# Deformable-convolution block on one core: 45 near taps, batched far columns, and an earlier silu

## The chip, the cores and the metric

The kernel runs on one core of one Trainium2 chip. The metric is the device time of one execution in microseconds (us); of several runs the median counts. The engines are called PE (TensorE), DVE (VectorE), ACT (ScalarE), POOL (GpSimd) and SP (SyncE, which here issues the large DMAs).

## The reference, cut to what matters

The block is a deformable convolution with a residual, then attention, then a mixture of experts. Only the first part is touched. For every pixel, each of 8 groups of 16 channels and each of 9 points, a small network gives an offset (x, y) and a softmax weight; the projected image is sampled at the shifted place with bilinear weights, and the 9 samples are added.

```python
N, H, W, C = (4, 32, 32, 128)
G, K = (8, 3)
P = K * K
...
x1 = jax.nn.silu(x1)
...
offset = x1 @ off_w + off_b
mask = jax.nn.softmax((x1 @ mask_w + mask_b).reshape(N, H, W, G, P), -1)
...
samples = _bilinear_sample(img, sg)
m = mask.reshape(N, H * W, G, P).transpose(0, 2, 1, 3).reshape(N * G, 1, H * W, P)
out = (samples * m).sum(-1)
...
return out @ out_w + out_b
```

## The kernel before

**Tiling.** The image is worked in 8 chunks (`CHUNKS`) of 4 rows (`ROWS`). A partition is one (column, image) pair, 32 by 4 = 128 of them, so a chunk has 4 rows times 8 groups = 32 places per partition.

**Near points as a stencil.** An offset of at most 2 pixels (`REACH`) moves a sample inside a window of 7 by 7 taps (`WIN`, `STENCIL` = 49). `prepare` (ACT) copies the offsets out of PSUM, squares them for the far test, and makes `hats`, the bilinear weight of each point on 5 taps in x and in y. DVE weighs the y hats with the softmax weights (`weigh_hats`), and in `stencils` multiplies them out for each of 9 points (`outer`, 800 elements) and adds that into the 7 by 7 stencil (800 elements). Then `products` (DVE) multiplies shifted copies of the image by the stencil, tap by tap, two taps in one instruction (a *unit*: 1024 elements, or 512 for the odd tap of each row; 28 units a chunk), into 7 slots of `prod`, and PE adds each tap up with 4 transposing matmuls (`add_up`).

**One turn.** DVE's `turn(k)` runs the products of chunk k as filling between the dependent steps of chunk k+1: `finish_silu`, `mask_logits`, `masks`, `weigh_hats`, 9 outer products and 8 additions. `own.wait()` in front of a step waits for DVE's own earlier results; `fill(n)` puts n units between. PE's `turn` puts into the taps, by their number, the count of far points (`AT_FAR`), the convolution of chunk k+2 (`AT_CONV`), the far part (`AT_SAMPLES`) and the projection (`AT_PROJECT`). All orders are written by hand.

**Far points.** A (row, group, point) column of a chunk in which any of the 128 partitions has an offset over 2 is *far*. DVE flags them (`off_most`, `far_flags`), PE counts them (`count_far`), ACT copies the counts (`count_out`), DVE lists up to 8 with one MAX8 (`list_far`), and POOL goes through the list in a loop of 7, column by column (`add_point`): position, cell, 4 indirect DMAs, weights, and the sum into `fix`. PE adds `fix` with `add_fix`.

**What ties POOL to the rest.** `list_far(k)` waits for `list_taken` = k, which POOL raises after the cast and the `place` update with which it begins chunk k-1, so after it has ended chunk k-2; and for `far_done`, which comes from `count_out(k)` on ACT, which waits for `fix_done`, also the end of chunk k-2. `fix_done` begins at 2, to let the first two through. `list_far(k+1)` stands in the DVE's `turn(k)`. PE's `add_fix(k-1)` stands in its `turn(k)` and waits for the end of POOL's chunk k-1.

Of the kernel before, what the change touches and what calls it, by code (L numbers as in the profile page):

```python
# [21 lines left out]
ALU = mybir.AluOpType  # L22
# [8 lines left out]
P = 128  # L31
# [24 lines left out]
ROW_UNITS = -(-WIN // 2)  # L56
UNITS = WIN * ROW_UNITS
# [28 lines left out]
FAR_UNIT = 8192.0  # L86

# [6 lines left out]
def first_of(unit):  # L94

    return unit // ROW_UNITS * WIN + unit % ROW_UNITS * 2
# [32 lines left out]
def hybrid_block_kernel(nc, x, in_w, in_b, out_w, out_b, off_w, off_b, mask_w, mask_b, dw_k, bn_g, bn_b,  # L129
                        bn_m, bn_v, attn_w, wr, br, w1, b1, w2, b2, gamma, beta, out):  # L130
    padded = nc.dram_tensor("padded", (WP, B, HP, C), F32, kind="Internal").ap()
    with ExitStack() as ctx:
# [3 lines left out]
        def sem(name):  # L136
# [24 lines left out]
        bias_parts = sb("bias_parts", [1, 3, 3 * GP + C], BF16)  # L161
# [23 lines left out]
        off_most = sb("off_most", [P, ROWS * GP])  # L185

        far = sb("far", [P, FAR_COLS], BF16)
        far_flags = far[:, :]
# [5 lines left out]
        far_xy = outer[:, :, :, :].rearrange("p g a b -> p (g a b)")[:, 0:ROWS * 2 * GP] \  # L194
            .rearrange("p (r o) -> p r o", r=ROWS)
# [27 lines left out]
        pos = sb("pos", [P, 2])  # L223
        low = sb("low", [P, 2])
        frac = sb("frac", [P, 2, 2])
        stride = sb("stride", [P, 2])
        cell_at = sb("cell_at", [P, 2])
        corner = sb("corner", [P, 4])
        cell_f = sb("cell_f", [P, 4])
        cell_now = sb("cell_now", [P, 4], U32)  # L230
        w_now = sb("w_now", [P, 2, 2])
        side = sb("side", [P, 2, 2])
        tap_d = sb("tap_d", [P, 2])
        tap_c = sb("tap_c", [P, 2, 2])
        within = sb("within", [P, 2, 2])
        got_sum = sb("got_sum", [P, 2, CG])
        got = sb("got", [P, 4, CG])
# [80 lines left out]
        square_done = sem("square_done")  # L318
# [14 lines left out]
        masks_done = sem("masks_done")  # L333
# [7 lines left out]
        gathered = sem("gathered")  # L341
# [75 lines left out]
        def _(sp):  # L417
# [62 lines left out]
            for k in range(HALF):  # L480
                s0, s1 = ROWS * k, (ROWS * (k + 1) if k < HALF - 1 else SLOTS)
                sp.wait_ge(prod_done, (k + 1) * STENCIL)
# [46 lines left out]
        def _(sc):  # L529
# [35 lines left out]
            def prepare(k):  # L565
# [10 lines left out]
                sc.activation(far_xy, raw[:, :, 0:2 * GP], ACT.Square).then_inc(square_done, 1)  # L576
# [15 lines left out]

            def copy_out(k):
# [12 lines left out]
            def clear_stencil(k):  # L606

                sc.wait_ge(prod_done, (k + 1) * STENCIL)
# [13 lines left out]
            prepare(0)  # L622
            count_out(0)
            silu(1)
            prepare(1)
            count_out(1)
            silu(2)
# [127 lines left out]
        def _(pe):  # L755
# [31 lines left out]
            def offsets(k):  # L787
                pe.wait_ge(x1_done, k + 1)

                pe.wait_ge(fold_done, 1)  # L790
                if not isinstance(k, int) or k > 0:
                    pe.wait_ge(square_done, k)
                for r in range(ROWS):
# [3 lines left out]
                mm.then_inc(off_mm, 1)  # L797
# [15 lines left out]
            for q in range(CHUNKS):  # L813
# [3 lines left out]
                if q == 2:  # L817
                    keep_clock(4, pair[0][:, 512:1024])
                    pe.wait_ge(bias_in, 16)
                    offsets(0)  # L820
# [11 lines left out]
            def count_far(k):  # L832

                pe.wait_ge(masks_done, k + 1)
# [3 lines left out]
                count = pair[1][:, 0:FAR_COLS]  # L838
                pe.matmul(count, ones16[:, :], far[:, :], start=True, stop=False)
                pe.matmul(count, ones[0:1, :], far_codes[:, :], start=False, stop=True).then_inc(far_mm, 1)  # L840
# [4 lines left out]
            def add_up(k, first, last):  # L845

                for i in range(first, last):
                    c, d = k + i // STENCIL, i % STENCIL
                    pe.wait_ge(prod_done, c * STENCIL + d + 1)
# [898 lines left out]
```

## Time and profile before

| | value |
|---|---|
| median of 3 runs | 697.59 us (697.52 to 699.57) |
| the profiled execution's own time | 699.83 us |
| its span | 698.0 us |
| busy, share of the span | PE 593.9 us (85%), DVE 583.2 us (84%), POOL 318.7 us (46%), ACT 227.5 us (33%) |
| DVE's first far list | at 61.2 us |
| DVE's turns begin | 63.88, 115.14, 165.22, 215.40, 265.80, 316.29, 366.50 us |
| last product of the convolution part | ends at 442.7 us |

The beginning of a turn is the start of its `finish_silu` (L1337). From 442.7 us on the kernel is the attention and expert part, whose code is the same in both kernels. A share of busy time over the whole span is a mean over those parts; for the change the turns have to be read alone.

### The profile page before, as it was taken

How to read it: one execution, taken by the hardware profiler on the slowest of the kernel's cores; microseconds unless marked ns; L12 is line 12 of the kernel's file. 1: busy time of each engine (PE TensorE's matmuls, PEld its weight loads, DVE VectorE, ACT ScalarE, POOL GpSimd, SP SyncE). 2: the span in 40 equal slices, each digit the busy share in tenths (PEclk: the TensorE clock that was granted, in tenths of full speed). 3: DMA queues.
4: the chain of work that ended last, by engine and by line, in shares of the span. 5: the costliest groups of instructions: out<-in, count | busy, mean ns of one | idle time of the engine just before them, and what ended most of it. 6: DMA issues, size and time to landing. Idle time of an engine off the chain costs nothing.

```text
span 698.0 us, 11520 instructions
## 1 busy us (share of the span) xinstructions
PE 593.9 (85%) x3630; PEld 444.2 (64%) x3630; DVE 583.2 (84%) x1068; ACT 227.5 (33%) x335; POOL 318.7 (46%) x332
## 2 busy tenths in 40 slices
PE   5988877879868968878878679889999999989995
PEld 4557656557556556556566557557777777776674
DVE  4589999999999999999999999816767776654877
ACT  6150502414314216107016000234454544424431
POOL 7507795897727795168278240201221211124322
PEclk9899999999999999999989899989999999999998
DMA  7096303003003006000000000000000000004211
GB/s 189 31 353 212 109 0 107 2 1 108 2 0 108 1 3 263 1 1 2 1 1 3 0 1 1 0 1 0 1 2 1 0 1 1 1 1 107 54 38 46
DMA packets 25724, 30.57 MB, mean 44 GB/s; under 512 B 5316, under 2 KB 17812, under 8 KB 25684
## 3 DMA queue, kind: packets, MB, share of 16 engines
q1 hardware_dynamic: 24094, 29.77, 13.1%
q0 software_dynamic: 896, 0.23, 0.4%
q8 instruction: 29, 0.48, 0.3%
q10 hardware_dynamic: 694, 0.01, 0.1%
q14 instruction: 11, 0.09, 0.0%
HBM read 24.94 MB, written 5.05 MB: 43 GB/s over the span
## 4 chain that ended last, share of the span: by engine, by line
PE 48%; DVE 25%; issue 12%; DVEq 2%; ACT 1%; DMA 0%; SPq 0%; POOL 0%; ACTq 0%; POOLq 0%
DVE prod L1481 11%; PE banks L851 11%; PE banks L967 8%; PE pair L947 8%; DVE outer L1418 4%; PE pair L1025 4%; DVE stencil L1424 4%; PE banks L957 4%; PE banks L1063 4%; PE pair L802 3%; PE pair L795 2%; PE banks L873 1%; DVEq L1481 1%; PE banks L939 1%; PE banks L918 1%
## 5 line engine op out<-in xcount | busy, mean ns | idle before, releaser
L851 PE MATMUL banks<-ident,prod 128*128 128x128 f32 x1568 | 222.9, 288 | 72.4 <-DVE prod L1481 70.1
L851 PEld LDWEIGHTS banks<-ident,prod 128*128 128x128 f32 x1568 | 184.0, 148 | 132.2 <-DVE prod L1481 108.2
L1481 DVE TENSOR_TENSOR prod<-shifted,stencil 128x1024 f32 (+1 forms) x224 | 238.2, 1086 | 5.3 <-PE banks L851 5.3
L1249 POOL TENSOR_TENSOR rstd_now<-mv_now,neg_half 128x2 f32<-128x2 f32 x32 | 23.0, 718 | 133.8 <-DVE mv_now L1533 133.8
L802 PE MATMUL pair<-xg,dw_diag 128*128 128x512 f32 x144 | 73.2, 609 | 0.3 <-DVE xg L1303 0.3
L1221 POOL CAST far_list_i<-far_list 1x8 int32<-1x8 f32 x8 | 33.7, 4217 | 74.9 <-DVE far_list L1467 47.0
L967 PEld LDWEIGHTS banks<-shifted 128*128 128x128 f32 x512 | 60.2, 192 | 8.1 <-issue 6.1
L967 PE MATMUL banks<-shifted 128*128 128x128 f32 x512 | 63.3, 277 | 2.3 <-ACT shifted L683 1.4
L947 PE MATMUL pair<-shifted 128*128 128x512 f32 x128 | 61.6, 604 | 0.7 <-ACT shifted L666 0.6
L1548 DVE TENSOR_REDUCE neg_max<-pair 128x1 f32<-128x1024 f32 x32 | 39.2, 1225 | 23.7 <-PE pair L947 22.6
L1418 DVE TENSOR_TENSOR outer<-hats 128x800 f32<-128x800 f32 x56 | 55.2, 986 | 0.5
L1424 DVE TENSOR_TENSOR stencil<-stencil,outer 128x800 f32 (+1 forms) x56 | 55.0, 982 | 0.0
L1186 POOL DMA_INDIRECT got<-padded,cell_now x28 | 45.4, 1621 | 8.4 <-issue 6.4
L585 ACT ACTIVATE hats<-off,tap_bias 128x576 f32 (+1 forms) x40 | 48.4, 1339 | 0.0
L678 ACT ACTIVATE shifted<-pair,neg_max 128x1024 f32<-128x1024 f32 x32 | 35.7, 1115 | 34.2 <-DVE neg_max L1548 34.2
L1553 DVE COPY shifted<-banks 128x512 f32<-128x512 f32 x32 | 22.0, 689 | 23.2 <-PE banks L957 23.2
L957 PE MATMUL banks<-ident,shifted 128*128 128x128 f32 x256 | 34.1, 277 | 0.0
L947 PEld LDWEIGHTS pair<-shifted 128*128 128x128 f32 x128 | 22.2, 193 | 17.4 <-issue 15.9
L1255 POOL TENSOR_TENSOR res<-res,bias_all 128x256 f32 x16 | 11.6, 728 | 46.2 <-DVE xg L1539 46.2
L558 ACT ACTIVATE gate<-pair,bn_fold 128x512 f32<-128x512 f32 x8 | 6.2, 774 | 79.7 <-issue 66.3
L957 PEld LDWEIGHTS banks<-ident,shifted 128*128 128x128 f32 x256 | 30.2, 144 | 1.3 <-issue 0.2
L1025 PE MATMUL pair<-shifted,stage 128*128 128x512 f32 x64 | 29.3, 597 | 1.4 <-DMA stage<-in_L_ffn_W_dram 1.4
(238 smaller groups left out, 895.0 us busy)
## 6 DMA issues: line engine op xcount, KB each, us to landing
shifted<-padded SPq DMA_DIRECT2D x42, 256.0 KB
shifted<-padded SPq DMA_DIRECT2D x14, 640.0 KB
res<-in_x_dram SPq DMA_DIRECT2D x4, 512.0 KB, 6.2
padded<-stage SPq DMA_DIRECT2D x4, 512.0 KB, 11.0
stage<-in_L_ffn_W_dram SPq DMA_DIRECT2D x16, 128.0 KB, 2.3
out_dram<-res SPq DMA_DIRECT2D x16, 128.0 KB, 1.8
padded<-stencil SPq DMA_DIRECT2D x2, 228.0 KB, 2.5
got<-padded,cell_now POOLq DMA_INDIRECT x28
```

The source lines that it names most:

```text
L585: own(sc.activation(hats[:, :, :, t].rearrange("p a (r g) -> p a r g", r=ROWS), off[:, bass.ds(k % OFFS, 1), :, 0:2 * GP].rearrange("p s r ...
L802: mm = pe.matmul(conv_bank.rearrange("c (r a) -> c r a", r=ROWS), dw_diag[:, t, :], src, start=(t == 0), stop=(t == 8))
L851: mm = pe.matmul(acc_of(c, r), prod[:, d % PROD, r * G:(r + 1) * G, :].rearrange("p g c -> p (g c)"), ident[:, :], is_transpose=True, star ...
L947: mm = pe.matmul(pair[s][:, h * 512:(h + 1) * 512], keyed[:, bass.ds(i * P, P)], normed_t[:, bass.ds((i // TILES) * TOK + h * 512, 512)], ...
L957: mm = pe.transpose(bank[h][:, m * P:(m + 1) * P], probs[:, s, (4 * h + m) * P:(4 * h + m + 1) * P], ident[:, :])
L967: mm = pe.matmul(bank[2][:, 0:C], probs_t[:, m * P:(m + 1) * P], normed[:, bass.ds((i // TILES) * TILES + m, 1), :].rearrange("p t c -> p ...
L1025: pe.matmul(pair[j][:, (f % 2) * 512:(f % 2 + 1) * 512], w1_sel[:, 2 * (q // 2) + j, (f % 2) * P:(f % 2 + 1) * P], normed2_t[:, q * 512:(q ...
L1186: gp.indirect_dma_start(out=got[:, a, :], out_offset=None, in_=table, in_offset=bass.IndirectOffsetOnAxis(ap=cell_now[:, a:a + 1], axis=0) ...
L1418: own(ve.tensor_tensor(to if q == 0 else outer[:, :, :, :], hy[:, :, q, :].unsqueeze(3).to_broadcast(full), hx[:, :, q, :].unsqueeze(2).to ...
L1424: own(ve.tensor_tensor(to, to, outer[:, :, :, :], ALU.add))
L1481: ins = ve.tensor_tensor(prod[:, dx:dx + n, :, :], shifted[:, dx:dx + n, bass.ds(((c % HALF) * ROWS + dy) * G, ROWS * G), :], stencil_of[: ...
L1548: ve.tensor_reduce(neg_max[:, s:s + 1], pair[s][:, :], AX.X, ALU.max, negate=True).then_inc(max_done, 1)
```

## The change

- **Taps**: the four corner taps of the window are dropped: 45 taps (`NEAR`) in a new order of rows (`ROW_ORDER`), 26 units a chunk instead of 28. A point whose weight falls on a corner tap now counts as far, and POOL's weights take it over.
- **Flags**: DVE's `off_most`, `far_flags` and ACT's square are gone. ACT makes two sign maps (`signs_of`), DVE two small instructions for the corners (`corners`), and PE's `count_far` sums them in six matmuls where two were. The four subtractions of the row maximum become one.
- **POOL**: columns are worked in batches of up to 4 (`add_batch`): take each, cells for all, gather each, weights for all, collect each. An absent column of a batch is skipped by a branch, but `cells` and `corner_weights` run once in a batch whatever its number. Further batches are skipped if empty.
- **Order**: `finish_silu` of the chunk after next moves from the turn's beginning into the stencil steps; the offsets of that chunk are computed at the end of PE's turn, so ACT begins the hats before the turn ends. `hats_used` is raised before the last addition. All but two additions are followed at once by an outer product, and two units stand behind each outer product. `list_far` stands one point earlier, `add_fix` at tap 21 in place of 35.

DVE, in `turn`, around the far list (L1418/L1526 is the outer product, L1424/L1534 the addition, L1481/L1591 a unit, MAX the far list, L1439 `finish_silu`). Before:

```order
L1418 TENSOR_TENSOR outer<-hats 128x800
L1481 TENSOR_TENSOR prod<-shifted,stencil 128x512
L1424 TENSOR_TENSOR stencil<-stencil,outer 128x32x5x5
L1481 TENSOR_TENSOR prod<-shifted,stencil 128x1024
L1467 MAX far_list<-pair 1x8
L1418 TENSOR_TENSOR outer<-hats 128x800
L1481 TENSOR_TENSOR prod<-shifted,stencil 128x1024
L1424 TENSOR_TENSOR stencil<-stencil,outer 128x32x5x5
```

DVE, the same place in the changed kernel:

```order
L1534 TENSOR_TENSOR stencil<-stencil,outer 128x32x5x5
L1578 MAX far_list<-pair 1x8
L1526 TENSOR_TENSOR outer<-hats 128x800
L1591 TENSOR_TENSOR prod<-shifted,stencil 128x512
L1591 TENSOR_TENSOR prod<-shifted,stencil 128x1024
L1534 TENSOR_TENSOR stencil<-stencil,outer 128x32x5x5
L1591 TENSOR_TENSOR prod<-shifted,stencil 128x1024
L1439 SCALAR_TENSOR_TENSOR gate<-gate,conv 128x512
L1526 TENSOR_TENSOR outer<-hats 128x800
```

The list moved one point forward, the units went from behind the additions to behind the outer products, and the silu came in.

POOL, the cell part of a column before:

```order
L1178 TENSOR_TENSOR pos<-off,place 128x2
L1179 ISA
L1179 TENSOR_TENSOR cell_f<-corner,place 128x4
L1180 TENSOR_SCALAR pos<-pos 128x2
L1181 TENSOR_SCALAR low<-pos 128x2
L1182 TENSOR_TENSOR cell_at<-low,stride 128x2
L1183 TENSOR_SCALAR cell_now<-cell_f,cell_at 128x4
L1186 DMA got<-padded,cell_now 128x16 x4
```

POOL, the cell part of a batch in the changed kernel:

```order
L1232 TENSOR_TENSOR pos<-got_off,got_at 128x8
L1233 TENSOR_SCALAR pos<-pos 128x8
L1234 TENSOR_SCALAR low<-pos 128x8
L1235 TENSOR_TENSOR cell_at<-low,stride 128x8
L1237 TENSOR_TENSOR cell_c<-cell_at 128x4
L1238 TENSOR_TENSOR cell_c<-cell_c,got_at 128x4
L1239 TENSOR_TENSOR cell_f<-corner,cell_c 128x16
L1241 CAST cell_now<-cell_f 128x16
L1242 ISA
L1311 COMPARE_AND_BRANCH
L1246 DMA got<-padded,cell_now 128x16 x4
```

Six instructions for one column became eight for up to four; four loads of codes and, for each present column, three copies (L1223 to L1225) stand ahead of them.

The diff, cut to its core:

```diff
+ROW_ORDER = (1, 0, 2, 3, 6, 4, 5)
+TAP_AT = [(dy, dx) for dy in ROW_ORDER for dx in range(WIN) if not (dy in (0, WIN - 1) and dx in (0, WIN - 1))]
+NEAR = len(TAP_AT)
...
-AT_FAR, AT_CONV, AT_SAMPLES, AT_PROJECT = 18, 22, 35, 39
...
-AT_LIST = 5
...
-STENCIL_FILL = (0, 1, 1, 0, 1, 1, 0, 1, 1)
-
-EXP_AT = 2
+AT_CONV, AT_FAR, AT_SAMPLES, AT_PROJECT, AT_OFFSETS = 4, 18, 21, 25, 32
+
+
+AT_LIST = 4
+
+
+AT_SILU = 5
+
+
+POINT_FILL = (1, 2, 2, 2, 2, 2, 2, 2, 2)
+STENCIL_FILL = (0, 0, 0, 0, 1, 0, 0, 0, 1)
+
+EXP_AT = 4
...
             def turn(j, conv_ahead):
+                prepare(j + 2)
                 clear_stencil(j)
-                prepare(j + 2)
-                count_out(j + 2)
+                signs_of(j + 2)
                 if conv_ahead:
                     silu(j + 3)
+                count_out(j + 2)
                 copy_out(j)
                 residual(j)
...
             def count_far(k):
 
-                pe.wait_ge(masks_done, k + 1)
+                pe.wait_ge(signs_done, k + 1)
+                pe.wait_ge(corners_done, k + 1)
...
+            def cells(n):
...
+            def gather(j):
...
+            def corner_weights(n):
...
+            def collect(k, group, j):
+                gp.wait_ge(gathered[j], 64)
...
+            def add_batch(k, j0, n):
+                codes = [gp.value_load(far_list_i[0:1, j0 + j:j0 + j + 1], min_val=0, max_val=MOST_CODE) for j in range(n)]
+                groups = [(code // GROUP_UNIT) % (ROWS * G) for code in codes]
+                for j in range(n):
+                    with gp.If(codes[j] > int(FAR_UNIT) - 1):
+                        take(k, (codes[j] // (G * GROUP_UNIT)) % ROWS * 3,
+                             (codes[j] % GROUP_UNIT).with_bounds(min_val=0, max_val=GP - 1), groups[j], j)
+                    gp.nop()
+                cells(n)
+                for j in range(n):
+                    with gp.If(codes[j] > int(FAR_UNIT) - 1):
+                        gather(j)
+                    gp.nop()
+                corner_weights(n)
+                for j in range(n):
+                    with gp.If(codes[j] > int(FAR_UNIT) - 1):
+                        collect(k, groups[j], j)
+                    gp.nop()
...
-                    with gp.Fori(0, LIST - 1) as j:
-                        code = gp.value_load(far_list_i[0:1, bass.ds(j, 1)], min_val=0, max_val=int(FAR_UNIT) * (P + 1) - 1)
-                        with gp.If(code > int(FAR_UNIT) - 1):
-                            add_point(k, (code // (G * GROUP_UNIT)) % ROWS * 3, (code % GROUP_UNIT).with_bounds(min_val=0, max_val=GP - 1),
-                                      (code // GROUP_UNIT) % (ROWS * G))
+                    for j0 in range(0, LIST - 1, BATCH):
+                        some = gp.value_load(far_list_i[0:1, j0:j0 + 1], min_val=0, max_val=MOST_CODE)
+                        with gp.If(some > int(FAR_UNIT) - 1):
+                            add_batch(k, j0, min(BATCH, LIST - 1 - j0))
...
+            def corners(k):
+                own.wait()
+                if not isinstance(k, int) or k > 0:
+                    ve.wait_ge(far_mm, k)
+                    ve.sem_inc(dve_waited, 1)
+                at = hats[:, :, :, :].rearrange("p a (g q) t -> p a g (q t)", q=PTS)
+                for kx in range(2):
+                    x0, y0 = (2 * 3 * TAPS + TAPS - 1) * kx, 2 * 3 * TAPS * kx
+                    last = ve.scalar_tensor_tensor(at_corner[:, :, kx, :], at[:, 0, :, x0:x0 + 2 * TAPS + 1:2 * TAPS], 0.0,
+                                                   at[:, 1, :, y0:y0 + 3 * TAPS:2 * TAPS + TAPS - 1], ALU.is_le, ALU.is_lt)
+                last.then_inc(corners_done, 1)
...
-                    if q == list_at:
+                    if q == AT_LIST:
                         list_far(k)
+                    if q == AT_SILU and silu_next:
+                        finish_silu(k + 1)
...
-                    fill(1)
+                    fill(POINT_FILL[q])
                     if q > 0:
                         own.wait()
+                        if q == PTS - 1:
+                            ve.sem_inc(hats_used, 1)
```

## Rows read from the trace of the kernel before

**Rows 1.** Busy us (instructions) of PE, PEld, DVE, ACT, POOL in one turn; PEclk.

```profile
115.14:165.22 50.08, 42.03 (x254) 31.37 (x253) 49.16 (x59) 14.82 (x15) 42.37 (x32) 0.93 0.12 38
```

**Rows 2.** DVE in order of time, masks: start us, us, line, operation, [idle before].

```profile
120.39 1.23 DVE L1481 TENSOR_TENSOR prod<-shifted,stencil 128x1024 f32 x1 [0.57 <-PE banks L851]
...
122.50 0.66 DVE L1351 TENSOR_TENSOR mask<-off,row_max 128x72 f32<-128x72 f32 x4
123.08 0.45 DVE L1357 TENSOR_TENSOR off_most<-outer 128x288 f32<-128x288 f32 x1
123.45 1.21 DVE L1481 TENSOR_TENSOR prod<-shifted,stencil 128x1024 f32 x1
124.58 0.30 DVE L1361 TENSOR_SCALAR far<-off_most 128x288 bf16<-128x288 f32 x1
...
130.04 1.66 DVE L1385 TENSOR_TENSOR hats<-hats,off 128x1440 f32<-128x1440 f32 x1
131.90 0.99 DVE L1418 TENSOR_TENSOR stencil<-hats 128x800 f32 x1 [0.20 <-DVE hats L1385]
```

**Rows 3.** DVE in order of time, stencil steps of the same turn.

```profile
142.47 1.21 DVE L1481 TENSOR_TENSOR prod<-shifted,stencil 128x1024 f32 x1
143.60 0.98 DVE L1424 TENSOR_TENSOR stencil<-stencil,outer 128x800 f32 x1
144.62 0.99 DVE L1418 TENSOR_TENSOR outer<-hats 128x800 f32<-128x800 f32 x1
145.53 0.68 DVE L1481 TENSOR_TENSOR prod<-shifted,stencil 128x512 f32 x1
146.13 0.98 DVE L1424 TENSOR_TENSOR stencil<-stencil,outer 128x800 f32 x1
...
148.17 0.45 DVE L1467 MAX8 far_list<-pair 1x8 f32<-1x288 f32 x1
```

**Rows 4.** ACT in order of time: two of the five hats, and the last hats step.

```profile
70.79 2.50 ACT L585 ACTIVATE hats<-off,tap_bias 128x576 f32<-128x576 f32 x2
...
77.33 2.70 ACT L591 ACTIVATE hats<-hats,tap_bias 128x2880 f32<-128x2880 f32 x1
```

**Rows 5.** POOL in order of time, beside the DVE steps of rows 3.

```profile
143.70 0.94 POOL L1196 TENSOR_TENSOR tap_c<-tap_c 128x4 f32<-128x4 f32 x1
144.72 0.95 POOL L1197 TENSOR_TENSOR w_now<-frac 128x4 f32<-128x4 f32 x1
...
148.39 6.75 POOL L1205 TENSOR_SCALAR within<-within 128x4 f32<-128x4 f32 x1
```

**Rows 6.** POOL in order of time, chunks 0 and 1, and the start of chunk 2.

```profile
61.86 6.75 POOL L1221 CAST far_list_i<-far_list 1x8 int32<-1x8 f32 x1 [3.59 <-DVE far_list L1467]
...
123.42 3.78 POOL L1178 TENSOR_TENSOR pos<-off,place 128x2 f32 x1 [2.26 <-issue]
...
162.12 0.36 POOL L1178 TENSOR_TENSOR pos<-off,place 128x2 f32 x1 [1.67 <-issue]
...
175.59 0.58 POOL L1190 TENSOR_TENSOR frac<-pos,low 128x2 f32<-128x2 f32 x1
...
186.52 0.70 POOL L1209 TENSOR_TENSOR got<-got,w_now 128x64 f32<-128x64 f32 x1 [0.30 <-POOL w_now L1206]
...
196.03 0.53 POOL L1221 CAST far_list_i<-far_list 1x8 int32<-1x8 f32 x1 [6.07 <-ACT far_counts L619]
```

**Rows 7.** POOL's indirect DMAs as a group: line, operation, count, busy us, mean ns.

```profile
L1186 POOL DMA_INDIRECT got<-padded,cell_now x28 | 45.4, 1621 | 8.4 <-issue 6.4 <-POOL cell_now L1183 2.0
```

**Rows 8.** DVE in order of time: the far list of turn 2.

```profile
198.79 0.45 DVE L1467 MAX8 far_list<-pair 1x8 f32<-1x288 f32 x1
```

**Rows 9.** POOL in order of time, while DVE runs its four small subtractions.

```profile
323.62 0.20 POOL L1190 TENSOR_TENSOR frac<-pos,low 128x2 f32<-128x2 f32 x1
323.77 0.20 POOL L1191 TENSOR_TENSOR tap_d<-low,place 128x2 f32<-128x2 f32 x1
```

**Rows 10.** DVE in order of time: the dense products at the end, 29 units.

```profile
413.97 28.73 DVE L1481 TENSOR_TENSOR prod<-shifted,stencil 128x512 f32 x29
```

More of the change, by code:

```diff
@@ L94, in first_of, with freed_by @@
 def first_of(unit):
-    return unit // ROW_UNITS * WIN + unit % ROW_UNITS * 2
+    return UNIT_AT[unit][0]
+def freed_by(tap):
+    dx = TAP_AT[tap][1]
+    before = [t for t in range(tap - NEAR, tap) if TAP_AT[t % NEAR][1] == dx]
+    return before[-1] + 1
 class Own:
@@ L591, in prepare, with signs_of @@
                 sc.activation(hf, hf, ACT.Relu, bias=tap_bias[:, TAPS:TAPS + 1], scale=-1.0).then_inc(hats_done, 1)
+            def signs_of(k):
+                raw = pair[0][:, :].rearrange("p (r o) -> p r o", r=ROWS)
+                if not isinstance(k, int) or k > 0:
+                    sc.wait_ge(far_mm, k)
+                    sc.sem_inc(act_waited, 1)
+                for i, sign in enumerate((1.0, -1.0)):
+                    last = sc.activation(signs[:, i, :, :], raw[:, :, 0:2 * GP], ACT.Sign,
+                                         bias=tap_bias[:, TAPS - 1:TAPS], scale=sign)
+                last.then_inc(signs_done, 1)
             def copy_out(k):
@@ L785, in _, with offsets @@
                       start=True, stop=True).then_inc(bias_mm, 1)
[L787 to L793, printed above, removed]
+            def offsets(k, r0, r1):
+                if r0 == 0:
+                    pe.wait_ge(x1_done, k + 1)
+                    pe.wait_ge(fold_done, 1)
+                    if not isinstance(k, int) or k > 0:
+                        pe.wait_ge(signs_done, k)
+                for r in range(r0, r1):
                     o = pair[0][:, r * 256:r * 256 + 3 * GP]
@@ L837, in count_far @@
                     pe.wait_ge(listed, k)
-                count = pair[1][:, 0:FAR_COLS]
-                pe.matmul(count, ones16[:, :], far[:, :], start=True, stop=False)
-                pe.matmul(count, ones[0:1, :], far_codes[:, :], start=False, stop=True).then_inc(far_mm, 1)
+                count = pair[1][0:1, 0:FAR_COLS]
+                by_corner = count.rearrange("p (g a b) -> p g a b", a=3, b=3)[:, :, 0:3:2, 0:3:2]
+                pe.matmul(count, ones[0:1, 0:1], far_codes[:, :], start=True, stop=False)
+                pe.matmul(by_corner, far_unit[:, :], at_corner[:, :, :, :], start=False, stop=False)
+                for i in range(4):
+                    mm = pe.matmul(count, far_unit[:, :], signs[:, i // 2, :, (i % 2) * GP:(i % 2 + 1) * GP],
+                                   start=False, stop=(i == 3))
+                mm.then_inc(far_mm, 1)
             def acc_of(c, r):
@@ L1158, in _ @@
             own(gp.memset(fix[:, :, :, :], 0.0))
+            for v in (got_off, got_at):
+                own(gp.memset(v[:, :, :], 0.0))
+            own(gp.memset(got_mid[:, :, :], 0.0))
+            own(gp.memset(tap_c[:, :, :, :, :], 0.0))
             own.wait()
@@ L1426, in stencils @@
                 own.wait()
-                ve.sem_inc(hats_used, 1)
             def first_stencils():
```

251 lines of the change are left out of this document (140 added, 111 removed).

## The prediction

> **What bounds the kernel now.** First the table of stretches: in a turn of 50.08 us DVE is busy 49.16 us, PE 42.03 and POOL 42.37 [rows 1]. In the convolution part DVE sets the pace, so an instruction less on DVE is worth its length, as long as PE and POOL follow. Then DVE in order of time: its only longer pauses are one wait for PE a turn, 0.57 us, and 0.20 us between hats and stencil [rows 2]. Last POOL in order of time. It is slower than its busy share says: it lists chunk 0 at 61.86 and is through with chunks 0 and 1 at 189.96, six us before its next start at 196.03 [rows 6]. DVE's list of turn 2, which needs exactly that, runs at 198.79 [rows 8]. So POOL ends just in time there: it has no slack behind DVE in turn 2.
>
> **What DVE saves.** From start to start a double unit costs 1.13 us, an addition or outer product 0.9, a single unit 0.60, and an addition followed at once by the outer product that waits for it 1.02, so 0.11 more [rows 3]. Per turn:
> - two double units fewer: -2.28.
> - four subtractions (0.66 busy, 0.58 to the next) become one of 288 elements, like the one of 0.45 busy, 0.37 to the next: -0.21. `off_most` and the flag go: -0.37 and -0.22 (0.30 less the 0.08 overlap) [rows 2].
> - two corner instructions of 64 elements, like a quarter of the 0.58: +0.30. Their wait for the hats takes the place of the stencil's 0.20.
> - six additions in place of two stand directly before an outer product: +0.44.
> - the wait for PE, 0.57, comes from a dense run of units behind the offsets; both are spread out now: -0.57 (the bounds are 0 and -0.57, and the nearest row is the place itself).
>
> Sum -2.9. The seven turns run from 63.88 to 416.85 (the start of the 29 dense units, 413.97, plus one single and two double units, 2.88 [rows 10]), so 50.4 on average; without turn 0, which is longer, 50.2, so 47.3 each in the changed kernel. The moved silu (0.60 us) leaves the last turn and enters the first stencils: turn 0 begins at 64.1 (no square before the first hats, corners and silu added; bounds 63.5 to 65). Turn 7 would begin at 64.1 + 7 x 47.3 - 0.6 = 394.6 and its 24 units (17 double, 7 single: 23.6) end at 418.2, against 442.7. **Alone that is -24.5 us.**
>
> **Work moved, and what hides it.** ACT begins the hats when DVE raises `hats_used`, before the last addition. Four hats 1.2 each [rows 4] end at 4.8; the exponential waits for the new subtraction, which ends 0.9 + 0.6 + 2.28 + 0.37 + 1.14 + 0.37 = 5.7 after the signal; then 0.45, a hat of 1.2 and the last step 2.7 [rows 4]: about 10.1. DVE needs the hats after those 5.7 and 0.60 + 1.14 + 0.37 + 1.14 + 0.75 + 0.60 = 10.3. A dead heat: 0 to 1 us a turn, I take 0. PE's moved work (nine convolution matmuls beside taps 4 to 12, offsets later) lies beside DVE's masks and hats; PE loses 16 transposes and gains four short matmuls in about 40 us of work, so it costs nothing while DVE stands at 47. The stencil's clearing and the signs come behind the hats on ACT and are needed later. The count of far points now waits for the corners, which are done before tap 12.
>
> **What POOL gets.** From the reference's inputs I counted the far columns of the 8 chunks: before 1, 2, 0, 2, 0, 1, 1, 0, together 7; the trace's 28 indirect DMAs, four a column, agree [rows 7]. With the corner condition: 1, 3, 2, 2, 0, 1, 2, 0, together 11. A column before takes 27.9 us (162.12 to 189.96: 13.5 until the weights, in them four DMAs, 10.9 for twelve weight instructions, 3.4 for the sum) [rows 6]. So a small POOL instruction costs 0.9 us beside DVE, and 143.70 and 144.72 show why: each ends just after DVE's next instruction begins (144.62, 145.53) [rows 3, 5]. One instruction per DVE instruction, whatever its size: that is what a batch saves. Behind the MAX8 at 148.17 one lasts 6.75 us, until the next pause of DVE in front of a waiting outer product [rows 3, 5]. In the changed order that next pause is nine DVE instructions behind the list: 8.8 us, a loss of about 8 once a turn. Now a chunk with n columns: cast and `place` 2.6; six loads of codes 6.3 (two and the branch took 2.26, an empty turn of the loop 6.07 / 5 = 1.2 [rows 6]); eight cell instructions 7.2; twenty of weights 18; branches and the second batch's load 3; and per column seven instructions 6.3, four DMAs 6.5 [rows 7] and 1.1 of waits. **That is 37 + 13.9 n: 51, 65 and 79 us for 1, 2 and 3 columns**, about 7 for none. Before it was about 12 + 28 n, 40 for one. Batches help from two on, but a chunk of two columns is not under one turn of 47.3.
>
> **Where it ends.** Chunk 0 starts at 64.1 and takes 51 + 8: 123. Chunk 1: 79 + 8: 210. DVE's list in turn 2 stands 22.8 us into the turn (masks 6.5, hats and corners 2.2, four outer products 3.6, three additions with gaps 3.0, seven units 7.4): 64.1 + 94.6 + 22.8 = 181.5. It is blocked, and behind it on DVE all units and steps. PE stands at tap 21 for the same chunk, ACT in `count_out`. But with DVE still, POOL is fast: its instructions last 0.20 and follow each other after 0.15 to 0.28 [rows 9]. Of the 28.5 us left, 3 for branches remain, 13.8 of sums become 5.1, 11.7 of weights 3.3, and cast and `place` 1.8: **wait 13**. Chunk 2 (two columns): 64 us from list to list against 47.3; 17 left become **9.5**. Chunk 3 the same, **9.5**. Chunks 4 and 5 (none, one) fit. Chunk 6 starts when 5 is done, about 375, ends at 375 + 65 + 8 = 448; PE wants it at tap 21 of the last products, about 438, DVE stands still from 441: **5**. Sum 37. So 697.6 - 24.5 + 37 = 710. The differences come from one execution of 699.8 us, 0.3% over the median; that does not matter to a difference. **I forecast 710 us.**
>
> The Trainium skill ("SBUF — State Buffer", section "SBUF: two separate sides") says that a VectorE instruction with two SBUF inputs and a GpSimd one lock a shared port pair for the whole instruction, and the loser fully blocks. The trace agrees for the instructions of 0.94 and 0.95 us; the one of 6.75 us lies across several of DVE's instructions, which the page does not say.
>
> **The rivals.**
> 1. *The long lock is one instruction, not a stretch*, so that it costs no 8 us a turn. Then chunk 1 ends at 194 and the waits are 7, 8, 8 and 0: 697.6 - 24.5 + 23 = 696, the same as before. Against it: 6.75 in both rows 5 and 6. The rule just named, read by the letter, gives this one. Chance 0.07.
> 2. *POOL waits little* (the other sign): loads without branches between them take 0.5 us, and ten us less a chunk. The waits are 6, 5, 5 and 0: 689. It turns faster where the waits together are under 24.5, that is where a chunk of two columns costs under 57 us. Against it the port pace, which no batch changes. Chance 0.16. At the far end no wait at all: 673.
> 3. *POOL costs more*: branches and address arithmetic of the skipped columns cost 1 us each, 10 us a chunk, which standing still does not shorten. Waits 28, 18, 18 and 10: 697.6 - 24.5 + 74 = 747; with half of it 728. Chance 0.15.
> 4. *DVE waits for ACT's hats*, 1 us in each of the four turns that POOL does not hold: 714. Chance 0.06.
> 5. *The change doesn't do what it says*: the corner flags find nothing new, seven columns remain, and the waits shrink to about 8: 681. Chance 0.03.
>
> **How the numbers follow.** The forecast has 0.53, with its own range 700 to 722. The range for 8 in 10 goes to rival 2's 689 and to 730, between the two values of rival 3. The bound for no change is 0.3%, 2.1 us, about what a measurement can tell. Faster: rivals 2 and 5 and the edge of rival 1, 0.21. Same: the rest of rival 1 and the forecast's lower edge, 0.07. Slower: 0.72.
>
> **What would show it.** Right: 44 indirect DMAs; DVE waits in front of the MAX8 in turns 2, 3 and 4, for POOL or for ACT's count, of 13, 9 and 9 us; PE idle in front of `add_fix`; undisturbed turns of 47.3 us; POOL instructions of 0.2 us in the waits and one of about 9 us behind a MAX8. Wrong: POOL gets from list to list with two columns in under 50 us, or DVE's pauses lie elsewhere (hats, `prod`). From the attention part on nothing should differ.

## The result and the profile after

| | before | after |
|---|---|---|
| median | 697.56 us (696.68 to 699.57, 4 runs) | 707.88 us (707.59 to 710.03, 4 runs) |
| span of the profiled execution | 698.0 us | 705.7 us |
| busy | PE 593.9, DVE 583.2, POOL 318.7, ACT 227.5 us | PE 587.9, DVE 563.8, POOL 371.2, ACT 233.9 us |
| last product of the convolution part ends | 442.7 us | 452.5 us |

The changed kernel is slower: ratio 1.0137, 95% interval 1.0116 to 1.0158. DVE lost 19.4 us of work and the kernel still became 10.3 us longer. Ratios and medians use fast executions alone, which leaves out a single one, of 1912 us, in the run with the residual moved behind the hats.

The experiments were timed in four groups, each with the kernel before beside it: 697.9, 699.6, 698.3 and 699.7 us in the order in which the groups were run. Times of different groups can therefore be compared only to about 2 us. Where less matters, the traces are compared: the last product of the convolution part, and DVE's waits. The part behind it varies by 3 us by itself (last section).

The table of stretches, one undisturbed turn (from row maximum to row maximum), in the columns of rows 1:

```profile
114.35:161.86 47.51, 40.90 (x242) 29.85 (x241) 46.95 (x55) 15.68 (x16) 35.13 (x34) 0.93 0.12 39
```

47.51 us in place of the 50.08 in rows 1: the saving on DVE is there. The waits between 60 and 460 us (engine, what it was about to write, line, for whom: us in total, times, longest) say where it went. First DVE, then PE:

```profile
DVE far_list L1578 <- POOLq L1328: 30.1, 3, 12.0
DVE at_corner L1488 <- DVE hats L1478: 1.3, 7, 0.2
```

```profile
PE banks L899 <- POOLq L1347: 34.8, 4, 13.5
```

POOLq L1328 is the mark that POOL has taken the previous list, L1347 the end of a chunk of `fix`. Beside this wait for POOL the list has only waits of DVE for its own results, each of 0.2 us at most. DVE in order of time, the far lists of chunks 2 to 5; rows 8 show that of chunk 3 (turn 2) in the kernel before:

```profile
137.65 0.45 DVE L1578 MAX8 far_list<-pair 1x8 f32<-1x288 f32 x1 [0.17 <-DVE stencil L1534]
...
196.94 0.45 DVE L1578 MAX8 far_list<-pair 1x8 f32<-1x288 f32 x1 [12.02 <-POOLq L1328]
253.18 0.45 DVE L1578 MAX8 far_list<-pair 1x8 f32<-1x288 f32 x1 [9.03 <-POOLq L1328]
309.42 0.45 DVE L1578 MAX8 far_list<-pair 1x8 f32<-1x288 f32 x1 [9.04 <-POOLq L1328]
```

From list to list it takes 56.24 us twice, 9 more than a turn: in these turns POOL's chunk of two columns is the clock of the kernel. POOL in order of time, when DVE's wait begins at 184.92 (196.94 - 12.02):

```profile
182.99 1.07 POOL L1264 TENSOR_TENSOR w_now<-frac 128x16 f32<-128x16 f32 x1
...
185.91 0.22 POOL L1274 TENSOR_TENSOR w_now<-w_now,got_off 128x16 f32<-128x16 f32 x1
186.09 0.21 POOL L1276 TENSOR_SCALAR reach<-reach 128x16 f32<-128x16 f32 x1
...
193.01 0.22 POOL L1291 TENSOR_TENSOR stage<-stage,got_sum 128x16 f32 x1 [0.42 <-POOL got_sum L1289]
195.16 0.18 POOL L1324 CAST far_list_i<-far_list 1x8 int32<-1x8 f32 x1 [1.93 <-ACT far_counts L649]
```

The same kind of instruction falls from about 1 us to 0.2 when DVE stands still. In rows 9 it was 0.2 too, but there DVE ran its four small subtractions: that it would be so in a standstill was an inference of the prediction, which this trace bears out. Behind the lists of chunks 1, 2 and 3 stand the long ones, where rows 5 had 6.75:

```profile
90.44 9.74 POOL L1246 DMA_INDIRECT got<-padded,cell_now  x1 [0.30 <-issue]
...
137.77 9.19 POOL L1225 COPY got_mid<-place 128x2 f32 x1
...
200.86 5.39 POOL L1223 COPY got_off<-off 128x3 f32 x1 [4.23 <-issue]
```

And the page's group that answers to rows 7, 44 indirect DMAs or 11 columns:

```profile
L1246 POOL DMA_INDIRECT got<-padded,cell_now x44 | 70.4, 1601 | 17.1 <-issue 11.6
```

### The profile page after: what moved, and what is told of

It is laid out like the page before. It is cut to its first block and busy times, and to the rows that moved or that the text cites. A ratio compares the mean times of both kernels' runs of the same rounds, so it can differ in the third digit from the quotient of the medians.

```text
span 705.7 us, 11135 instructions
## 1 busy us (share of the span) xinstructions
PE 587.9 (83%) x3518; PEld 438.2 (62%) x3518; DVE 563.8 (80%) x1028; ACT 233.9 (33%) x343; POOL 371.2 (53%) x432
## 5 line engine op out<-in xcount | busy, mean ns | idle before, releaser
L892 PE MATMUL banks<-ident,prod 128*128 128x128 f32 x1440 | 218.8, 297 | 54.4 <-DVE prod L1591 52.3
L892 PEld LDWEIGHTS banks<-ident,prod 128*128 128x128 f32 x1440 | 177.7, 152 | 112.3 <-DVE prod L1591 85.8
L1591 DVE TENSOR_TENSOR prod<-shifted,stencil 128x1024 f32 (+3 forms) x208 | 216.0, 1076 | 0.1
L1246 POOL DMA_INDIRECT got<-padded,cell_now x44 | 70.4, 1601 | 17.1 <-issue 11.6
L1526 DVE TENSOR_TENSOR outer<-hats 128x800 f32<-128x800 f32 x56 | 55.7, 994 | 1.2
L1534 DVE TENSOR_TENSOR stencil<-stencil,outer 128x800 f32 (+1 forms) x56 | 55.4, 989 | 0.0
L899 PE MATMUL banks<-ident,stage 128*128 128x128 f32 x32 | 6.8, 351 | 34.8 <-POOLq L1347 34.8
L1223 POOL COPY got_off<-off 128x3 f32 x11 | 15.8, 1439 | 28.9 <-issue 25.7
```

Of the source, the lines that this page charges most:

```text
L892: mm = pe.matmul(acc_of(c, r), prod[:, slot, r * G:(r + 1) * G, :].rearrange("p g c -> p (g c)"), ident[:, :], is_transpose=True, start=(t ...
L1246: gp.indirect_dma_start(out=got[:, j, a, :], out_offset=None, in_=table, in_offset=bass.IndirectOffsetOnAxis(ap=cell_now[:, j, a:a + 1], a ...
L1526: own(ve.tensor_tensor(to if q == 0 else outer[:, :, :, :], hy[:, :, q, :].unsqueeze(3).to_broadcast(full), hx[:, :, q, :].unsqueeze(2).to ...
L1534: own(ve.tensor_tensor(to, to, outer[:, :, :, :], ALU.add))
L1591: ins = ve.tensor_tensor(prod[:, dx:dx + n, :, :], shifted[:, dx:dx + n, bass.ds(((c % HALF) * ROWS + dy) * G, ROWS * G), :], stencil_of[: ...
```

## The experiments

Each is the changed kernel with the edit shown, if nothing else is said. The theory on trial is the prediction's: DVE's saving is real, and POOL's chunks, slowed beside DVE and locked out behind each list, for 9 us where DVE did not wait at it, take more than it gives.

**POOL works no column.** The edit leaves the far points' work out.

```diff
-                            add_batch(k, j0, min(BATCH, LIST - 1 - j0))
+                            gp.nop()
```

> The changed kernel, but POOL works on no far column (the batches are left out, so the contribution of the far columns is missing); all flags, counts and lists stay. Theory (DVE saves about 22 us, and POOL's columns cost 30 us of waits in front of the far list): the three waits of 12.0, 9.0 and 9.0 us vanish and nothing takes their place, 707.9 - 30.1 = 678 us. Rival (the waits only cover another wait for the hats, for PE's freed slots or for ACT, which would come in their place): 690 us or more.

Measured: 677.93 us (676.93 to 679.38), ratio to the kernel before 0.9704 (0.9658 to 0.9749). DVE's waits for POOL in front of the far list are gone. The largest wait of DVE in the convolution part, which now ends at 421.3 us, is this one:

```profile
DVE at_corner L1488 <- DVE hats L1478: 1.3, 7, 0.2
```

So POOL's columns cost 707.9 - 677.9 = 30.0 us, and DVE's waits in the trace were 30.1. No other wait took their place, so the rival is out. What the change costs besides is the later start of turn 0, which is in this run too (66.5 us; below).

**The same in the kernel before**, `add_point` left out:

> The kernel before, with POOL working on no far column (their contribution is missing). Theory (POOL was just in time before, at 198.5 against 198.8 us in turn 2, and costs nothing): within 0.3% of 697.6 us. Rival (POOL's instructions, by the shared port or by the list, already cost time before): under 694 us.

Measured: 698.91 us, ratio 1.0007 (0.9985 to 1.003). In the kernel before the columns were free. With both kernels rid of them the change is worth 698.9 - 677.9 = 21.0 us (both of one group); the kernel before hid 7 columns, the changed one pays 30 us for 11.

**Without the corner flags**, so that the 7 columns of before remain; the corner taps' weight is left out of the result:

```diff
-                pe.matmul(by_corner, far_unit[:, :], at_corner[:, :, :, :], start=False, stop=False)
```

> The changed kernel with the corner map left out of PE's count: points on a corner tap are no longer far, so their corner weight is missing; 7 columns as before (28 indirect DMAs) in the new batches. Theory (the four extra columns make the waits): chunk 1 has two columns and is about 13 us earlier at the list of turn 2, of the wait of 12 us 5 remain; chunk 2 has none, so turns 3 and 4 don't wait: 707.9 - 25 = 683 us. Rival (the batched form itself is too slow, whatever the number of columns): two or three waits remain, 695 us or more.

Measured: 685.79 us (0.9815; 0.9771 to 0.9858). One wait is left, in turn 2:

```profile
DVE far_list L1577 <- POOLq L1327: 6.9, 1, 6.9
```

The four additional columns cost 707.9 - 685.8 = 22.1 us, the seven others 7.9. The theory's figure was 683 with 5 us of wait left; the rival, that the batched form is too slow by itself, had two or three waits and 695 or more.

**Batches of one**, `BATCH` = 1 in place of 4:

> The changed kernel with batches of one column (BATCH = 1), so that cells and weights run once for each column. Theory (a small POOL instruction costs one DVE instruction's time, 0.9 us, whatever its size, and a third as much while DVE stands still): 27 us more of fixed work for each further column, some 22 us more wait at the list of turn 2, 9 each in turns 3 and 4, 5 to 8 in the last products, 750 us. Rival (loading the codes and the branches are what costs, batching is no help): 712 us or less.

Measured: 779.33 us (1.1156; 1.1092 to 1.1219), above both figures. The waits of DVE in the convolution part, which now lasts beyond the window of 460 us, are mainly these two (60 to 530 us):

```profile
DVE far_list L1578 <- POOLq L1328: 86.1, 3, 38.1
DVE prod L1591 <- PE banks L892: 16.9, 2, 16.4
```

The expectation had 34 + 18 + 18 for the lists, and they were 38.1, 23.9 and 24.1, with 16.9 for PE in the last products, which itself waited for POOL (16.0 us in front of `add_fix`). So batching is not what hurts: without it the kernel takes 71 us more. I had put its worth too low.

**The list three points later**, at point 7 of the stencil steps (the expectations of this run and later ones call it tap 7), where DVE's next pause comes sooner:

```diff
-AT_LIST = 4
+AT_LIST = 7
```

> The changed kernel with DVE's far list at point 7 in place of 4 (AT_LIST = 7), add_fix still at tap 21. By the trace the list then stands about 17 us later in the turn. Theory A (the long POOL instruction behind the list lasts until DVE's next pause in front of a waiting outer product): behind the list of point 7 that pause is outer product, two units and addition away, so POOL's long instruction shrinks from about 9 us to about 4. Theory B (PE holds back too: at tap 21 it waits for the same chunk and frees no slots): the wait moves from the list to the products (DVE waits for PE), so that turn 2 still loses some 8 to 12 us; with POOL 5 us a turn faster the total is 5 to 12 us under 707.9: 699. Rival (the list alone is the bound): 17 us less, 691 us; rival (the lock is one instruction, its length has nothing to do with the place): POOL's long instruction stays at 9 us, 705 or more.

Measured: 702.70 us (1.0047; 1.0028 to 1.0065). POOL in order of time behind the list of chunk 1, then DVE's waits:

```profile
104.76 3.77 POOL L1268 TENSOR_SCALAR tap_c<-tap_c 128x16 f32<-128x16 f32 x1
```

```profile
DVE prod L1591 <- PE banks L892: 24.0, 3, 8.3
```

The time lies between the theory's 699 and the 705 of the rival. The long instruction is 3.8 us where it was 9.7, so its length goes with the place of DVE's next pause. The wait for the list is gone, but 24.0 of 30.1 us came back on another resource: DVE's products wait for slots of `prod` that PE frees, and PE stands at `add_fix` for the same POOL chunk.

**The far term twelve taps later** (list where it was):

```diff
-AT_CONV, AT_FAR, AT_SAMPLES, AT_PROJECT, AT_OFFSETS = 4, 18, 21, 25, 32
+AT_CONV, AT_FAR, AT_SAMPLES, AT_PROJECT, AT_OFFSETS = 4, 18, 33, 37, 32
```

> The changed kernel with PE's add_fix at tap 33 in place of 21 and the projection at taps 37 to 43 in place of 25 to 31, the list still at point 4. Theory (the list is the wait that ends last in turns 2 to 4, PE's wait lies beside it): no gain, 706 to 710 us. Rival (PE's wait at tap 21 is what counts): 8 us or more less.

Measured: 719.13 us (1.0264; 1.0229 to 1.0299), 11 us slower than the changed kernel. Neither theory had that. The waits of DVE, and ACT in order of time at the end of turn 1:

```profile
DVE far_list L1578 <- POOLq L1328: 26.8, 3, 10.9
DVE hats L1478 <- ACT hats L610: 5.5, 5, 1.1
DVE row_sum L1464 <- ACT mask L603: 5.1, 5, 1.3
```

```profile
161.84 0.60 ACT L634 ACTIVATE res<-banks 128x512 f32 x1 [10.05 <-PE banks L914]
162.49 0.89 ACT L592 ACTIVATE off<-pair 128x864 f32 x1
163.49 4.65 ACT L604 ACTIVATE hats<-off,tap_bias 128x576 f32 x4
```

ACT's residual waits for the projection and stands ahead of the next chunk's offsets and hats in ACT's order. With the projection at the turn's end it holds the hats, and DVE gets two new waits of about 1 us in each of five turns. With 1.3 us for row maxima these are 11.9 us of new waits, against 3.3 less at the list: 8.6 us more. The last product ends at 463.4 us, 10.9 later than in the changed kernel; 0.9 of the rest is a later start of turn 0 (67.9 against 67.0), and 1.4 us are not explained.

**Both places late**: list at point 7, far term at taps 33 and 37.

> The list at point 7 and add_fix at tap 33, together. Theory (two waits for the same POOL chunk, each of which alone holds the turn): only now the 12 us wait of turn 2 goes, since there are about 14 us more until either is due, and POOL is 5 us a turn faster behind a shorter lock; in turns 3 and 4 POOL needs about 60 us for two columns against 47.5 a turn, so 3 to 9 us of each remain: 707.9 - 12 - 6 = 690 us (686 to 697). Rival (POOL's rate alone decides, the place doesn't matter): 705 or more.

Measured: 699.11 us (0.9994; 0.9971 to 1.0017), a miss by 9. The waits of DVE:

```profile
DVE far_list L1578 <- POOLq L1328: 9.8, 2, 4.9
DVE hats L1478 <- ACT hats L610: 5.4, 5, 1.1
DVE row_sum L1464 <- ACT mask L603: 5.1, 5, 1.4
DVE row_max L1449 <- ACT off L592: 1.3, 4, 0.6
```

The list costs 9.8 in place of 30.1, and the hats 11.8 that the expectation had at nothing: again the residual.

**The residual behind the hats**: as the last, with ACT's `residual(j - 1)` behind turn j's `prepare`, and chunk 0's exponential early.

```diff
-                    if t == EXP_AT:
+                    if t == (2 if isinstance(k, int) and k == 0 else EXP_AT):
...
+                if not isinstance(j, int) or j > 0:
+                    residual(j - 1)
...
-                residual(j)
```

> The run with both late places (the list's MAX8 at tap 7, sampling and last products of the far term at taps 33 and 37) still held DVE for 11.8 us on hats and their sums and row maxima, and for 9.8 us on the far list. Here ACT takes the residual of a turn only behind the work that it does for the chunk after next, so that the late projection no longer stands ahead of the hats in ACT's order; chunk 0 also has its exponential behind the second hat (worth 2.0 us by the run that tried it alone). Theory (ACT's residual, waiting for the late projection, held the hats): the waits on hats, row sums and row maxima fall to about nothing, 12 us go, 2 us for the exponential, and 1 to 5 us come back as a longer wait for the list, since POOL's chunks now have shorter turns: 699 - 12 - 2 + 3 = 688, between 685 and 692. Rival (the waits on hats come of the hats' own length, not of the residual ahead of them): the waits stay at about 2 us a turn and the time is 697. Second rival (POOL's chunks alone set the time by now): the hats' waits go and as much comes back at the list, 697 too, with list waits near 20 us.

Measured: 692.21 us (0.9915; 0.9887 to 0.9942), 0.2 us above the expected range. The last product ends at 436.7 us, in the last run at 447.6. Of DVE's waits in the convolution part this one is left at the top, and those for hats, row sums and row maxima are gone:

```profile
DVE far_list L1581 <- POOLq L1331: 13.8, 2, 6.9
```

So it was the residual that held the hats. Of the 11.8 us, 4.0 came back at the list: with shorter turns POOL's chunk is due sooner.

**The far term at taps 30 and 33**, else as the last:

> As the run before, but with the far term's sampling and last products at taps 30 and 33 in the place of 33 and 37. If DVE's time is set by POOL's chunks through the list of far positions, POOL's stage of a chunk is now waited for earlier, by 3 to 4 taps of about 1 us, and PE's wait for POOL's last product reaches DVE in up to three turns: 688 + 3 x (0 to 2) = 688 to 694. If instead the late place of the products costs something of its own at the end of the turn, it is below 688.

Measured: 691.69 us (0.9913; 0.9888 to 0.9939), within the first theory's range. It is the lowest time of a complete kernel in the study, but the runs can't tell it from the last one: the last product ends at 436.4 and 436.7 us. The waits stand at the products now:

```profile
DVE prod L1594 <- PE banks L895: 14.6, 5, 7.6
```

**The far term at taps 27 and 29**, list at point 7, chunk 0's exponential early, the residual in its old place:

> List at tap 7, sampling and last products at taps 27 and 29, exponential of chunk 0 behind the second hat, the residual where it was. The run with the list at tap 7 alone took 702.7 with three waits of 7.5 to 8.3 us of DVE on PE's products, which wait for POOL's last product. Four taps later is about 4 us a turn more room for POOL: if the waits are paid afresh in each turn, they fall to about 3.5, 4.3 and 4.3, 12 us less, 2 less for the exponential: 689. If only the slack counts once (POOL is late by a fixed pace), the first wait falls by 4 and the others stay at 8: 702.7 - 4 - 2 = 697. The residual's wait moves by 4 us towards the hats too and may hold them by up to 1 us a turn: 697 to 701 then.

Measured: 702.57 us (1.0054; 1.0031 to 1.0078), above all three figures. DVE in order of time, the products behind whose wait the turns 2 and 3 go on:

```profile
197.09 1.23 DVE L1591 TENSOR_TENSOR prod<-shifted,stencil 128x1024 f32 x1 [3.21 <-PE banks L892]
...
254.01 1.23 DVE L1591 TENSOR_TENSOR prod<-shifted,stencil 128x1024 f32 x1 [8.42 <-PE banks L892]
256.68 1.23 DVE L1591 TENSOR_TENSOR prod<-shifted,stencil 128x1024 f32 x1 [1.44 <-PE banks L892]
```

With the far term at 21 these waits were 7.5, 8.3 and 8.3. Four taps of room helped the first wait by 4.3 and the others not at all, and while PE catches up short second waits of 0.9, 1.4 and 1.7 us appear; the sum is 24.1 where it was 24.0. The earlier exponential did show: the last product ends at 446.7 us against 448.3. The part behind it took 1.4 us longer (254.0 against 252.6), which hid that in the time. Here the later deadline was slack that counted once; in the turns that POOL paces it brought nothing.

**Chunk 0's exponential early, alone** (the first two lines of the diff above):

> The changed kernel with the exponential of chunk 0 after the second hat, as before, and after the fourth for the others. DVE waits 2.76 us for it in front of the first row sum, and its turn 0 begins 2.9 us later than forecast. Theory (that wait is on the path into the first turn): 2 to 3 us less, 705.3 us, if POOL's chain moves along with it. Rival (hidden, because POOL's chain or the projection holds the start): 707 to 709 us.

Measured: 705.92 us (1.0081; 1.0056 to 1.0107). That is 2.0 less, as expected, but between two groups and so no more than their spread. The trace is the better witness: the wait in front of chunk 0's row sum falls from 2.76 to 0.57 us, turn 0 begins at 65.5 us in place of 67.0, and the three waits at the list are the same 30.1.

**A pause of DVE behind the MAX8.** One line is added: DVE waits for its own MAX8.

```diff
                 ve.max(far_list[:, :], pair[1][0:1, 0:FAR_COLS]).then_inc(listed, 1)
+                ve.wait_ge(listed, k + 1)
```

> The changed kernel with one wait more: DVE waits for its own MAX8 (0.2 us) before it goes on to the outer product. Nothing else moves; eight pauses cost 8 x 0.2 = 1.6 us. Theory (POOL is locked out from DVE's first two-input instruction behind the MAX8 until DVE's next pause, nine instructions later; a pause at once ends it): the POOL instructions of 9.74, 9.19 and 9.05 us behind the lists become 1 to 2 us, POOL gains some 8 us a chunk at its slow pace, which is 3 to 4 us of DVE's wait at its fast one (with the list at tap 7, 5.5 us less lock took 2.1 us off a wait): the waits 12.0, 9.0 and 9.0 become 5, 5.5 and 5.5, together 14 less, 1.6 more for the pauses: 707.9 - 12.5 = 695, between 688 and 699. Rival (the MAX8 itself starts the lock, or a pause counts only after several two-input instructions): the long instructions stay near 9 us, and the time is 708 to 710.

Measured: 695.48 us (694.64 to 696.87), ratio 0.9944 (0.9928 to 0.9959): one *additional* wait makes the changed kernel 12.4 us faster, and by 0.4% to 0.7% faster than the kernel before. The pause was not tried together with the moved residual. DVE, then POOL, in order of time at the list of chunk 2, the place of the 9.19 us above:

```profile
138.89 0.46 DVE L1578 MAX8 far_list<-pair 1x8 f32<-1x288 f32 x1 [0.17 <-DVE stencil L1534]
139.38 0.99 DVE L1526 TENSOR_TENSOR outer<-hats 128x800 f32<-128x800 f32 x1
140.29 1.82 DVE L1592 TENSOR_TENSOR prod<-shifted,stencil 128x512 f32 x2
```

```profile
137.93 1.62 POOL L1246 DMA_INDIRECT got<-padded,cell_now  x1 [0.30 <-issue]
139.85 1.34 POOL L1246 DMA_INDIRECT got<-padded,cell_now  x1 [0.30 <-issue]
141.49 1.44 POOL L1246 DMA_INDIRECT got<-padded,cell_now  x1 [0.30 <-issue]
```

The outer product starts 0.49 us behind the MAX8 instead of 0.38, and over the very same stream of DVE instructions POOL gets through. No POOL instruction of the convolution part from the first list on is over 2.6 us any more. DVE's waits:

```profile
DVE far_list L1578 <- POOLq L1328: 15.6, 3, 6.9
```

1.7, 6.9 and 6.9 where 5, 5.5 and 5.5 were expected: the sum (15.6 for 16) was right, its parts were not.

## Why the prediction held, point by point

The forecast was 710 us and the time is 707.9.

- **DVE's saving.** Forecast: turns of 47.3 us; measured 47.5. From the row maximum of turn 0 (66.97) to that of turn 6 (381.48) there are 314.5 us, less the 30.1 of waits 47.4 each. The forecast has a slip of 0.1 here: the turns before, without turn 0, take (416.85 - 115.14) / 6 = 50.3 on average, not 50.2, and 50.3 - 2.9 is the 47.4 that came. "Alone" the change was to bring 24.5 us, with the last product at 418.2; the two runs without columns say 21.0, and without them the last product ends at 421.3. Most of this is the next point's 2.9 us.
- **The start of turn 0.** Forecast 64.1, at most 65; it was 67.0. This step failed. I moved the exponential behind the fourth hat in every turn and priced it only where DVE has units to fill with. In the prelude it has none. DVE in order of time, chunk 0's row sum:

```profile
39.38 0.45 DVE L1464 TENSOR_REDUCE row_sum<-mask 128x32 f32<-128x288 f32 x1 [2.76 <-ACT mask L603]
```

  Undone alone it took 2.2 us off this wait and made turn 0 begin 1.5 us earlier; the rest of the 2.9 us stays open.
- **The hats: a dead heat, taken as 0.** ACT, then DVE, in order of time in turn 1:

```profile
118.18 2.70 ACT L610 ACTIVATE hats<-hats,tap_bias 128x2880 f32<-128x2880 f32 x1
```

```profile
120.98 1.66 DVE L1478 TENSOR_TENSOR hats<-hats,off 128x1440 f32<-128x1440 f32 x1
```

  The hats end at 120.88 and are used at 120.98: no wait, and 0.1 us of room. That rival 4 was near is shown by the runs with the late projection, where one ACT instruction ahead of the hats cost 12 us in all.
- **What POOL gets.** 11 columns, as counted. The formula 37 + 13.9 n, with the 8 for the lock that the forecast added, gives 73 for chunk 6 (two columns, no wait of DVE in it); POOL in order of time shows its cast and its end:

```profile
371.96 0.31 POOL L1324 CAST far_list_i<-far_list 1x8 int32<-1x8 f32 x1 [2.21 <-issue]
...
378.66 0.67 POOL L1223 COPY got_off<-off 128x3 f32 x1 [4.24 <-issue]
...
405.55 7.72 POOL L1254 TENSOR_TENSOR cell_at<-pos,low 128x8 f32<-128x8 f32 x1
...
437.84 0.73 POOL L1291 TENSOR_TENSOR stage<-stage,got_sum 128x16 f32 x1 [0.43 <-POOL got_sum L1289]
```

  From cast to last sum these are 66.6 us. The columns' own work agrees: copies 5.4, eight DMAs 14.5 and two sums 8.6 are 28.5 us, and 2 x 13.9 is 27.8. What I had too high is the part that does not depend on n. The loads of codes were to cost 6.3 and the gap that holds five of the six is 4.24; the eight cell instructions took 6.4 with their wait, not 7.2; the twenty weight instructions 24.0 with the 7.72 of the one behind the list in it, not 18 + 8. And the 3 us of branches and the second batch's load come after the last sum, where nobody waits for them but POOL's next chunk.
- **The lock.** Forecast 8.8 us, from MAX8 to DVE's next waiting outer product; measured 9.74 and 9.19. Behind the lists that DVE had waited for, POOL was in its loads for half of the stretch, and 5.39 us were left (the copy at 200.86). Rival 1 said that the long instruction is no stretch of DVE's stream and that the kernel would then take 696. The mechanism of rival 1 fell: the length follows the distance to the pause (9.2 with the list at point 4, 3.8 at point 7, none with a pause at once). With the lock taken away the kernel takes 695.5, but that this is the rival's figure is luck: it had 23 us of waits, and 15.6 came.
- **The waits.** Forecast 13, 9.5, 9.5; measured 12.0, 9.0, 9.0. The fourth, 5 us before the last products, did not come. PE in order of time at that `add_fix`:

```profile
439.88 0.66 PE L899 MATMUL banks<-ident,stage 128*128 128x128 f32 x4 [0.23 <-POOLq L1347]
```

  Chunk 6 was through at 438.6 instead of 448: 6.4 us from the terms above, and 3.0 because it began at 372.0 and not at 375.
- **The sum.** Forecast end of the products: 418.2 + 37 = 455.2; +2.9 for the start, -6.9 for the waits (30.1 in place of 37), +1.3 for the rest, of which the slip of 0.1 in seven turns is 0.7: 452.5. Errors of opposite sign made the total better than its parts; that the 707.9 came within 2.1 us of the forecast is in part luck. The mechanism, which wait stands where and for what, was right but for the fourth wait.
- **The other rivals.** 2 (POOL waits little, 689) had a load at 0.5 us; the gap with five loads, their arithmetic and a branch is 4.24, so at most 0.85 each. It needed under 57 us for a chunk of two columns, and chunk 6 took 66.6, or 58.9 without its long instruction of 7.72: not far off. 3 (skipped branches cost 1 us each) has no sign in the trace: POOL's idle time before the cells, behind the branches, is 0.98 us in chunk 0 with three absent columns, 0.52 in chunk 6 with two and 0.34 in chunk 1 with one. 5 (nothing flagged, 681) is measured as 685.8 by the run without corner flags: the seven columns cost 7.9 where I had 8, and 2.9 of the 4.8 us of difference are the start of turn 0.
- **From the attention part on nothing should differ.** It took 705.7 - 452.5 = 253.2 us in place of 255.3; see the last section.

## What to carry to other kernels

When the engine that sets the pace gets faster, ask of every side engine how long one of its units of work takes against the new turn, not how busy it is on average: POOL was at 46% of the span and had no slack behind one list, and the change gave it 57% more columns and 6% less time. A hand-off with a single buffer carries such a delay from turn to turn. Four taps more room for it took 4.3 us off the first wait and nothing off the later ones, while a shorter chunk, without the lock, took 10.3, 2.1 and 2.1 us off the three. Whoever moves a waiting instruction later must read what stands behind it on its own engine: here one residual on ACT cost 12 us of new waits, and taking it out of the way (with the exponential of chunk 0 early, and the far term at taps 30 and 33) made a complete kernel of 691.7 us, 0.87% faster than before (interval 0.61% to 1.12%).

## What the runs showed of the hardware

- **A lock over many instructions.** Beside DVE's stream of two-input instructions a small POOL instruction takes the length of one DVE instruction. Behind a MAX8 it takes as long as DVE does not pause: 9.74 and 9.19 us in the changed kernel, 3.77 with the list at 7, 6.75 in the kernel before [rows 5, 6]. A wait of DVE for its own MAX8, which moves the next instruction by 0.11 us, ends it. A pause of DVE is not the only end, nor a MAX8 the only beginning: the cast at 67.21 us in the changed kernel, behind the first list, took 3.47 us and ended as DVE began the row sum, with no idle time of DVE there, and in the kernel before 3.78 us at 123.42 [rows 6] and 2.81 us at 166.07 lie across several DVE instructions with no MAX8 ahead. The Trainium skill ("SBUF — State Buffer", section "SBUF: two separate sides") has the lock for a single instruction; these runs agree for the ordinary ones, and differ behind a MAX8 and in these two places. What starts such a stretch was not tried further and stays open.
- **TensorE's clock behind the convolution part.** The attention and expert part has the same code in both kernels, and in the two profiled executions it was 2.1 us shorter after the change. That is no effect of the change on it. Counted from the end of the last product, one execution each:

| run | part behind the last product | mean granted clock, first 20 us | next 40 us |
|---|---|---|---|
| kernel before | 255.3 us | 0.99 | 0.92 |
| changed kernel | 253.2 us | 0.91 | 1.00 |
| changed, no columns | 255.4 us | 1.00 | 0.91 |
| residual behind the hats | 255.5 us | 1.00 | 0.91 |
| far term at 30 and 33 | 252.6 us | 1.00 | 1.00 |
| pause behind the MAX8 | 252.5 us | 1.00 | 1.00 |

  1.00 is the upper of the two levels, 2.4 GHz; 0.91 means that a part of the stretch ran at 1.2. The part is longest where the lower clock falls into the 40 us, in which PE is busy for over 38 us in every row, and shortest where neither stretch has it; the other variants lie within the same 252.5 to 255.5 us. So 3 us of a kernel's time go with where the lower clock falls, and variants of the same kernel differ by that. In the 30 us before the end of the last product the mean was 1.00 before and 0.91 after, and DVE's units, which pace that stretch, followed each other without a gap in both. What decides when the clock falls was not tried.
